# Row sums moved from VectorE to ScalarE with a second, row-major reading of the matrix, and GpSimd's tensor work moved to VectorE

## The reference

```python
def cxin_conv(x, a, eps, W, b):                # three dense layers
    ax = a @ x
    h = ax + (1.0 + eps[0]) * ax
    for i in range(3):
        h = relu(h @ W[i].T + b[i])
    return h
# layer 0
m = concatenate((cxin_conv(x, adj, eps1, W1, b1), cxin_conv(x2, adj, eps2, W2, b2)), axis=1)
x = layernorm(x + m @ Wm.T + bm)
# layer 1
A_hat = adj + eye(4096)
deg = sum(A_hat, axis=1)
d = where(deg > 0, rsqrt(deg), 0)
out = (d[:, None] * A_hat * d[None, :]) @ x
x = layernorm(x + out @ W.T + b)
```

## Time and profile before

| | |
|---|---|
| timed runs | 649.15, 649.18, 649.63 us, median 649.18 |
| span of the profiled execution (no other time of it is given) | 647.4 us |
| busy TensorE, VectorE, ScalarE, GpSimd | 601.5, 562.9, 364.9, 272.1 us |
| read from memory | 139.14 MB |
| mean granted TensorE clock | 0.989 of full speed |

### The profile page before, as it was taken

How to read it: one execution, slowest core, us unless ns; L and a number is a source line. 1 busy time by engine, 2 the same in 40 slices (tenths; PEclk the granted TensorE clock), 3 DMA queues, 4 the chain that set the end, 5 groups by cost and what they waited for, 6 DMA issues and landing times.

```text
span 647.4 us, 8346 instructions
## 1 busy us (share of the span) xinstructions
PE 601.5 (93%) x2692; PEld 485.3 (75%) x2692; DVE 562.9 (87%) x564; ACT 364.9 (56%) x441; POOL 272.1 (42%) x167
## 2 busy tenths in 40 slices
PE   5949999899999999999999999899989999999984
PEld 4738888678888878888878887557757878878863
DVE  5939998997999998899899799974799988988974
ACT  5514536562353773353675244175786787787772
POOL 0553606780340591160384159960465042340171
PEclk9969999999999999999999999999999999999998
DMA  8943753425536435336534473576588989999800
GB/s 298 413 177 121 269 195 131 175 91 190 189 137 240 149 130 194 130 130 230 183 141 159 162 292 125 199 281 237 196 296 328 359 338 402 344 353 376 320 33 34
DMA packets 21287, 141.54 MB, mean 219 GB/s; under 512 B 2320, under 2 KB 2832, under 8 KB 5008
## 3 DMA queue, kind: packets, MB, share of 16 engines
q1 hardware_dynamic: 20544, 139.15, 58.0%
q10 hardware_dynamic: 720, 2.10, 0.8%
HBM read 139.14 MB, written 2.10 MB: 218 GB/s over the span
## 4 chain that ended last, share of the span: by engine, by line
PE 27%; POOL 24%; issue 22%; DVE 21%; ACT 5%; DMA 1%; POOLq 0%; DVEq 0%; SPq 0%; ACTq 0%
PE ps L332 19%; DVE alo L625 13%; POOL hlo L774 6%; PE pd L350 3%; ACT ahi L482 3%; POOL rstd L790 3%; DVE rowsum L636 2%; POOL x1lo L860 2%; PE pd L362 2%; DVE rowsum L640 2%; POOL xb L780 2%; POOL xb L783 2%; POOL x1lo L822 2%; POOL yt L815 1%; POOL vareps L788 1%
## 5 line engine op out<-in xcount | busy, mean ns | idle before, releaser
L625 DVE TENSOR_TENSOR alo<-raw,ahi 128x1024 fp32r<-128x1024 f32 x255 | 356.0, 1414 | 61.3 <-ACT ahi L482 60.0
L482 ACT ACTIVATE ahi<-raw 128x1024 fp32r<-128x1024 f32 x255 | 267.6, 1059 | 248.1 <-PE ps L332 231.1
L332 PE MATMUL ps<-ahi,x1hi 128*128 128x512 f32 x504 | 163.7, 401 | 34.5 <-DVE alo L625 13.5
L332 PE MATMUL ps<-ahi,x2s 128*128 128x512 f32 x512 | 159.9, 391 | 0.0
L332 PE MATMUL ps<-alo,x1hi 128*128 128x512 f32 x504 | 158.9, 392 | 0.0
L332 PE MATMUL ps<-ahi,x1lo 128*128 128x512 f32 x504 | 158.7, 391 | 0.0
L332 PEld LDWEIGHTS ps<-ahi,x1hi 128*128 128x128 f32 x504 | 92.1, 189 | 66.4 <-issue 26.1
L332 PEld LDWEIGHTS ps<-ahi,x2s 128*128 128x128 f32 x512 | 97.0, 189 | 20.5
L332 PEld LDWEIGHTS ps<-ahi,x1lo 128*128 128x128 f32 x504 | 95.2, 189 | 20.3
L332 PEld LDWEIGHTS ps<-alo,x1hi 128*128 128x128 f32 x504 | 95.2, 189 | 19.9
L774 POOL TENSOR_TENSOR hlo<-h,hhi 128x512 fp32r<-128x512 f32 x36 | 79.2, 2233 | 68.8 <-ACT hhi L487 68.8
(11 more groups left out here) (66 smaller groups left out, 367.1 us busy)
## 6 DMA issues: line engine op xcount, KB each, us to landing
raw<-a_t SPq DMA_DIRECT2D x124, 1024.0 KB, 4.8
raw<-a_t SPq DMA_DIRECT2D x7, 512.0 KB, 8.8
xn<-x SPq DMA_DIRECT2D x3, 1024.0 KB, 8.6
out<-outn ACTq DMA_DIRECT2D x3, 512.0 KB, 5.4
par<-params SPq DMA_DIRECT2D x1, 708.0 KB, 14.2
xn<-x SPq DMA_DIRECT2D x2, 256.0 KB, 4.6
raw<-a_t SPq DMA_DIRECT2D x2, 256.0 KB, 5.1
xn<-x SPq DMA_DIRECT2D x1, 512.0 KB, 8.2
```

The costliest lines, as they stand in the source:

```text
L332: mm = pe.matmul(ps[bank][:, :], block_of(w, n), a[c], start=(n == 0 and k == 0), stop=(n == JB - 1 and k == 2))
L482: act.activation(ahi[:, n % SPLIT, :], raw_tile(layer, n), ACT.Copy).then_inc(hi_ready, 1)
L625: dve.tensor_tensor(alo[:, n % SPLIT, :], raw_tile(layer, n), as_f32(ahi[:, n % SPLIT, :]), ALU.subtract).then_inc(lo_ready, 1)
```

## The change

1. adj is handed over a second time, row-major (`rows`), as 64 chunks of 128 rows x 2048 columns, 1 MB each. SP loads a chunk behind each pair (into two buffers), and ScalarE copies it onto itself with `accum_out`, two pairs behind the tiles. VectorE adds the two halves of each row. The row sums of `raw`, the column of ones and TensorE's 8 degree matmuls per quarter (16 instructions in the trace) are gone. A pair of `raw` is now free when its low part is made (`lo_ready`).
2. GpSimd keeps only the constants and the powers (`rstd`, `degpow`). The rest of its list is VectorE's, as whole quarters instead of halves. ScalarE rounds y of all quarters.
3. y of quarters 0 to 2 is made inside quarter 3 of layer 0 (steps 12 to 30), y of quarter 3 at steps 22 to 24 of layer 1, quarter 0. The base of layer 1 is written onto `xn`. Diagonal tiles get their identity three blocks ahead.
4. The shift of a normalisation is one operation; quarter 3 of layer 0 and the quarters of layer 1 are unrolled.

```diff
+DVE_BASE = (10, 7)
+DVE_SHIFT = tuple(k + 2 for k in DVE_AGGREGATE)
+DVE_MAKE_Y = (KB + 4, 2 * KB + 4, 3 * KB + 4, 22)
+ACT_ROUND_Y = tuple(k + 1 for k in DVE_MAKE_Y)
+DVE_SPLIT_Y = tuple(k + 2 for k in DVE_MAKE_Y)
+AHEAD = 3
 # sync
             def load0(g, s):
-                sp.wait_ge(raw_used, g * RAW + (s + 1 - RAW))
+                sp.wait_ge(lo_ready, g * (2 * RAW) + 2 * (s + 1 - RAW))
                 load(raw[:, s], g * RAW + s).then_inc(raw_in[s], 16)
+            def load_rows(g, s):
+                wait(sp, row_summed, g * RAW + (s + 1 - ROWBUFS))
+                sp.dma_start(rowbuf[:, s % ROWBUFS, :], src).then_inc(row_in[s % ROWBUFS], 16)
 # tensor
             def merge(q):
-                for k in range(KB):
-                    pe.matmul(degree[:, k:k + 1], rowsum_all[:, k * P:(k + 1) * P], ones[:, :],
-                              start=(k == 0), stop=(k == KB - 1), skip_group_check=True)
 # scalar
+            def sum_rows(q, n, layer=0):
+                if n % 2 == 0 or (isinstance(q, int) and (layer, q, n // 2 < LAG) in ((0, 0, True), (1, 0, False))):
+                    return
+                s = n // 2 - LAG
...
+                line = rowbuf[:, s % ROWBUFS, :]
+                act.activation(line, line, ACT.Copy, accum_out=part).then_inc(row_summed, 1)
+            def round_y(g):
+                act.wait_ge(yt_ready, g + 1)
+                act.wait_ge(block_used, (QUARTERS - 1) * JB + KB * (g + 1))
+                act.activation(x1hi[:, g, :], yt[:, :, :].rearrange("p k d -> p (k d)"),
+                               ACT.Copy).then_inc(yhi_ready, 1)
 # vector
-            def sum_rows(q, n):
...
+            def split_h(q, l, m):
+                wait(dve, hhi_ready, q * (LAYERS * M) + (M * l + m + 1))
+                dve.tensor_tensor(hlo[:, m, :], h[:, m, :], as_f32(hhi[:, m, :]),
+                                  ALU.subtract).then_inc(hlo_ready, 1)
+            def shifts(done, r=slice(0, KB)):
+                wait(dve, rstd_ready, done)
+                dve.scalar_tensor_tensor(out=nshift[:, r], in0=mv[:, r, 0], scalar=-1.0, in1=rstd[:, r],
+                                         op0=ALU.mult, op1=ALU.mult).then_inc(norm_ready, 1)
+            def make_y(g):
+                dve.wait_ge(xn_ready, 2 * (g + 1))
+                dve.wait_ge(d_ready, g + 1)
...
+            def add_identity(q, n):
+                wait_raw1(dve, q, n)
...
+                dve.tensor_tensor(square, square, identity[:, :], ALU.add).then_inc(identity_added, 1)
```

More of the change, by code:

```diff
@@ L157, in build @@
         lo_half = sem("lo_half")
-        rowsum_step = sem("rowsum_step")
-        raw_used = sem("raw_used")
+        row_in = [sem(f"row_in{i}") for i in range(ROWBUFS)]
+        row_summed = sem("row_summed")
+        deg_step = sem("deg_step")
         block_used = sem("block_used")
@@ L279, in _ @@
             groups = QUARTERS * PAIRS // RAW
+            for s in range(ROWBUFS):
+                load_rows(0, s)
             for g in (1, 2):
@@ L289, in _ @@
                 load0(groups - 1, s)
+                load_rows(groups - 2, s)
                 if s == 1:
@@ L585, in _ @@
             act.activation(whi[:, :], par[:, 0:WM_AT], ACT.Copy).then_inc(whi_ready, 1)
-            with act.Fori(1, QUARTERS) as q:
+            with act.Fori(1, QUARTERS - 1) as q:
                 layer0_quarter(q, q - 1)
+            layer0_quarter(QUARTERS - 1, QUARTERS - 2)
             layer1_quarter(0, None)
-            with act.Fori(1, QUARTERS - 1) as q:
+            for q in range(1, QUARTERS):
                 layer1_quarter(q, q - 1)
-            layer1_quarter(QUARTERS - 1, QUARTERS - 2)
             last = QUARTERS - 1
@@ L614, in split_a @@
             def split_a(q, layer, n):
-                if layer == 0 and n == 0 and isinstance(q, int):
+                if layer == 0 and n == 0 and isinstance(q, int) and q == 0:
                     for c in range(CH):
@@ new lines, in residual_base, with residual_bias, residual @@
+            def residual_base(q):
+                dve.tensor_tensor(xb[:, :, :], as_f32(quarter(x1hi, q)), as_f32(quarter(x1lo, q)),
+                                  ALU.add).then_inc(xb_step, 1)
+            def residual_bias(q):
+                wait(dve, xb_step, q + 1)
+                dve.tensor_tensor(xb[:, :, :], xb[:, :, :], bias_rows(BM_AT), ALU.add).then_inc(xb_ready, 1)
+            def residual(q):
+                wait(dve, merge_done, q + 1)
+                wait(dve, xb_ready, q + 1)
+                wait(dve, xn_ready, q * 2)
+                dve.tensor_tensor(z[:, :, :], merged, xb[:, :, :], ALU.add).then_inc(z_ready, 1)
@@ L654, in statistics_taken @@
             def statistics_taken(done):
-                wait(dve, stats_step, done * KB)
+                wait(dve, stats_step, done)
             def aggregate(blocks=range(KB), last=None):
@@ L840, in prepare_layer1, with degree_power @@
-            def prepare_layer1(q):
-                wait(pool, z_ready, q + QUARTERS)
-                dq = dall[:, q, :] if isinstance(q, int) else dall[:, bass.ds(q, 1), :].rearrange("p o k -> p (o k)")
-                pool.tensor_copy(dcur[:, :], dq).then_inc(xb_step, 1)
-                pool.tensor_tensor(xb[:, :, :], quarter(xn, q), bias_rows(BO_AT), ALU.add).then_inc(xb_ready, 1)
-            pool.memset(ones[:, :], 1.0).then_inc(const_ready, 1)
+            def degree_power(q):
+                wait(pool, deg_ready, q * 2 + 2)
+                pool.tensor_tensor(degpow[:, :], degc[:, :], halves[:, :], ALU.pow).then_inc(degpow_ready, 1)
```

322 lines of the change are left out of this document (143 added, 179 removed).

## The result

The changed kernel takes 626.58 us (median of five runs, 625.29 to 632.05) against 649.47 for the kernel before (649.15 to 649.81): a ratio of 0.966, 95% interval 0.9625 to 0.9695. 618.8 was forecast, in a range of 610 to 636. The profiled execution of after is its slowest run, 632.05 us with a span of 630.0; the other four have spans of 623.3 to 625.5. So where its trace is compared with the forecast span of 617.0, there are 13.0 us to explain, of which 7.8 are in the median.

A forecast was written before the change was run, and what follows sets the result against it. TensorE's own work was taken as the floor, with VectorE late in single places because of GpSimd. Gains of 1.9 + 4.4 + 5.0 + 8.9 + 4.5 + 2.9 + 2.8 = 30.4 took 649.18 to 618.8 us, range 610 to 636.

The forecast's parts named there:

- The main mechanism: VectorE is late in single places because of GpSimd beside it; forecast A, 618.8 us, chance 0.62.
- the 0.3 left for jitter in a middle quarter: Middle quarters of layer 0 go to 99.1 us plus 0.3 for jitter, gaining 2 x 2.5 = 5.0 us.
- Row sums at 1.92 us, covered on ScalarE: Layer 0: each 2048-column sum costs ScalarE 1.92 us, bounds 1.7 and 3.84, hidden under TensorE's time.
- Rival E: Accumulating costs more than copying, so ScalarE bounds layer 0 and the kernel gets slower, about 671 us at worst; chance 0.06.
- Quarter 0: 1.9 gained: Quarter 0 of layer 0: 11.6 us lost now go, late row chunks cost 9.7; bounds 11.6 gained, 10 lost.
- each chunk 5.1 us after the last as two transfers alternate: Quarter 0: row chunks land at this rhythm after chunk 0 at 25 us, x's last two pieces another 2.5 each.
- Quarter 1 to its merge: 38.3 forecast: Layer 0, quarter 1 to its merge: falls from 42.7 to 38.3 us, 4.4 gained.
- 62.7 instead of 61.1: Last merge of the loop to layer 1: falls from 70.0 to 61.1 us with y made earlier, 8.9 gained.
- rival D: Start of layer 0: ScalarE stuck at first chunks lets the clock fall, or loads are slower; 10 us more, 629; chance 0.08.
- Rival B: Transfers bind layer 0: at 361 GB/s a pair takes 5.81 instead of 5.44 us; 645 us; chance 0.10.
- Rival C: VectorE becomes the pace of layer 1 and eats 10.2 us of gains; 629 us; chance 0.12.
- The last y: Layer 1, quarter 0: block 24 waits about 3 us for y; projection starts 43.5 us after the merge, 4.5 gained.

The follow-up runs named there:

- Experiment 1: Kernel before with one half of the change each: row sums moved to ScalarE alone, 634.61 us; GpSimd's tensor work moved to VectorE alone, 618.25 us.
- experiment 2: Changed kernel without row chunk transfers, ScalarE summing zeros: 611.92 us; changed kernel without transfers and sums of quarter 0's 16 chunks: 614.07 us.
- experiment 5: Changed kernel without adding the identity to diagonal tiles in quarters 1 to 3 of layer 1: 624.01 us.
- Experiment 3: Changed kernel with step 1's row sum behind step 2's evacuation, in quarters 1 to 3 of layer 0 and quarter 0 of layer 1: 622.63 us.
- experiment 4: Changed kernel with quarter 0's chunks starting at block 13: 641.33 us; spread version, ten chunks in quarter 0 and 18 in each other quarter: 641.84 us.

## Why the prediction was right, and where it was off

*The main mechanism held, as one half of a pair.* VectorE was late, in quarter 0 and at each merge, because it had the row sums and GpSimd beside it (split 1414 to 1221 ns; 101.9 to 99.1 from merge to merge). The forecast put it down to GpSimd alone. Experiment 1 shows that either half removes it: with the row sums gone and GpSimd as before the split is still 1399 ns, and the middle quarters come to 99.1 and 99.7. In layer 1, which has no row sums on VectorE before either, only GpSimd's half helps: the last stretch takes 57.6 us with the row sums moved alone (57.5 before) and 54.9 with GpSimd's work moved alone. The terms from there on miss by 0.3 to 1.6 us each; the 0.3 left for jitter in a middle quarter wasn't needed.

*Row sums at 1.92 us, covered on ScalarE.* 1.91, and 0.18 for reading the accumulator, which no row had shown. Covered: in experiment 2, without the transfers, TensorE is busy for 392.0 of the 392 us from 8 to 400, under all the sums. Rival E falls by this.

*Quarter 0: 1.9 gained was wrong.* It lost 2.0 in the trace, a miss of 3.9 (3.0 in the trace of experiment 5). The step that failed is "each chunk 5.1 us after the last as two transfers alternate". The waits of ScalarE for its chunks are as forecast at first (8.2 us, then TensorE idle for 3.8 at 30, forecast 3 near 26), but the chunk after next is summed at 39.5, 14 us after the first instead of 10.2, and the row sum of step 1 of quarter 1 starts at 107.1 where this rhythm gives 101.5. SP's order has three pairs of tiles between the second chunk and the third, not one, and that alone makes 3.7 of the 5.6 us. From there on a chunk comes every 5.0 to 5.4 us, as forecast, and 7.5 and 8.0 where a piece of x is between; the last took 6.6. In bytes it is the same: the pairs that SP asks ahead were missing from the count (44.9 MB instead of 38). The rate had been taken well: 413 forecast, 407 over the whole quarter. Counted on TensorE instead, its five waits are 10.2 us where 9.7 were charged, close in sum only by luck (3.4 at the end instead of 1.0, less in the middle), and the slow matmuls behind the first wait (12 in 5.1 us from 29.9, worth 2.7) had been charged nothing.

*Quarter 1 to its merge: 38.3 forecast, 41.6 measured.* No wait is in it, but blocks at the lower clock, behind 3.4 us of idle time. In the trace of experiment 5, with 2.8 us of idle time and the full clock behind them, it takes 39.4: most of this miss belongs to the profiled run. The forecast had seen the sum ahead of the evacuation and charged it as 1.0 us inside quarter 0; it hadn't charged the clock behind it. The same happens at the start of layer 1 (62.7 instead of 61.1, and 23.1 instead of 21.5 for what follows: 2.0 idle, then 4.57 us for two blocks worth 2.73). That is rival D's mechanism, in a place where D didn't look for it, and it coexists with the main one. Experiment 3 takes both waits away, and 4.0 us with them. It doesn't split the price of the clock from that of the waits; for the trace of after the rows do, 3.4 idle and 3.2 slow.

*Rival B, transfers bind layer 0:* not in the middle quarters of the change (339 GB/s, 99.1 us), yes in quarter 0. The Trainium skill (DMA: Bandwidth & Descriptors, Where 436 GB/s comes from) would have reads of HBM bound near 358 GB/s. The trace doesn't agree: 423 over 8 us, 407 over 102.

*Rival C, VectorE paces layer 1:* in part. The two stretches are 1.2 us over each, 2.4 in all, and leaving the additions out gives 1.4 and 0.8 (experiment 5). Their price was nearly right (0.19 on the chain, 0.17 put down); the room for them was not. In the second stretch they fall on the steps with the statistics, behind seven steps of 1.40: 1.14 + 0.40 + 0.19 = 1.73 us of VectorE for a block that TensorE does in 1.365. The forecast had worked it out for quarter 1 alone, on the steps with residual2, at 1.57.

*The last y:* TensorE waits for it at 465.2 us for 1.6, 2.9 with the waits beside it, as forecast (about 3).

The misses add up: 3.9 + 3.3 + 1.6 + 1.6 + 0.6 + 1.2 + 1.2 + 0.3, less 0.6 for the middle quarters, is 13.1, the span's 13.0. What the forecast didn't ask is whether both halves are needed. It gave the row sums' move a share of the gain; alone it has one (15.1 us), beside the other half it is a loss of 8.3, and kept out of quarter 0 it is a gain again (618.25 to 613.67; the three degree columns that go are 5.0 us by their price, so they account for all of it).

Open: how much of a run's spread comes from the clock. Kernels with chunks in quarter 0 spread by 1.8 to 6.8 us between runs, the changed ones without by 0.5 to 2.3, and the kernel before, which has an idle time of 9.3 us there, by 0.7 to 3.8. The profiled run of after is 5.5 us over its median with a mean clock of 0.983 (0.988 to 0.991 in the others). Of the change itself only this run has a trace; that of experiment 5 says that the same place costs 3 us more or less from run to run. What decides it isn't known. Open too: what moving y, the single shift and the unrolled quarters give by themselves.

## What to carry to other kernels

When two changes relieve the same engine, test each alone: the second may only add its cost. A second reading of the operand is free where TensorE's time per tile covers the transfers, and dear in the filling phase, where the prefetch of the next stage must be counted too; count bytes up to the time, not per pair. In an in-order queue, a wait for a transfer must never stand ahead of what frees TensorE's accumulators, because 2 to 3.4 us of idle TensorE cost up to as much again in clock here.

## What the runs showed of the hardware

- GpSimd's two-input operation of 128x1024 takes 15.62 us beside back-to-back VectorE operations and 2.39 beside VectorE with gaps.
- A ScalarE copy of 2048 columns with accumulation takes 1.91 us (1.92 is the estimate from copies of 512 and 1024 columns without accumulation), and 0.18 for a separate read of the accumulator.
- In after the granted clock was 0.69, 0.61 and 0.79 over the 8 us behind idle times of 3.8, 3.4 and 2.0 us (from 29.9, 110.6 and 413.2); behind the 2.5 us wait of experiment 3 it was 0.79 from 29.3 to 37.3. Behind 2.8 us of idle time at 109.7 in experiment 5 it was 1.00, and so it was behind single waits of 0.5 to 1.4 us in quarter 0 of after. The length of the idle time alone doesn't tell whether the clock falls.
- A chunk of 1 MB lands 7.8 us after its issue (median of after) when tiles are in the same queue, 18.6 at most. Two buffers then carry one chunk per 5 us; in the spread version of experiment 4 (7.7 us) ScalarE waits for chunks though the share of the DMA engines is 0.85.
